# The last update of each level's outermost tile given to ScalarE and GpSimd, in the stages of three and two groups

## The reference

```python
def step(g, inp):
    ci, ni, nm, nc = inp
    local = g[:, ci, :]
    nb = g[:, ni, :]
    neigh = (nb * nm[None, :, None]).sum(axis=1) / nc
    u = jnp.concatenate([local, neigh], axis=-1)
    y_sc = jnp.tanh(u @ w1 + b1) @ w2 + b2
    g = g.at[:, ci, :].set(local + y_sc[:, None] * w_y[None, :])
    return (g, None)
```

## Time and profile before

| what | value |
|---|---|
| median of 3 runs | 4584.73 us (4581.04 to 4588.59) |
| the profiled execution | 4616.78 us, its span 4615.0 us |
| TensorE clock granted in it, mean | 0.974 |
| busy over the span | PE 4300.1, DVE 3981.3, ACT 2602.7, POOL 2142.3 us |
| scan, seven to four groups (from the first dot) | 2965.2 to 4220.5 us |
| scan, three groups (32 levels) | 4220.5 to 4396.5 us |
| scan, two groups (32 levels) | 4396.5 to 4535.6 us |
| scan, one group and the end | 4535.6 to 4615.0 us |

### The profile page before, as it was taken

How to read it: one execution, slowest core, us unless ns; L and a number is a source line. 1 busy time by engine, 2 the same in 40 slices (tenths; PEclk the granted TensorE clock), 3 DMA queues, 4 the chain that set the end, 5 groups by cost and what they waited for, 6 DMA issues and landing times. The chain is left out here.

```text
span 4615.0 us, 62189 instructions
## 1 busy us (share of the span) xinstructions
PE 4300.1 (93%) x20842; PEld 3332.0 (72%) x20842; DVE 3981.3 (86%) x5650; ACT 2602.7 (56%) x4500; POOL 2142.3 (46%) x1696
## 2 busy tenths in 40 slices
PE   5999999999999999999999999988888888889977
PEld 4888888888888888888888888744444444555555
DVE  7999999999997999999999997577777777788888
ACT  4666666666666666666666665433333333334463
POOL 1565443444343334434443434455555555555544
PEclk8999999999999999999999999998988999999999
DMA  4444444444444444444444444698898888888763
GB/s 120 146 139 145 150 138 147 138 147 144 143 143 142 145 141 147 139 146 141 146 141 140 145 140 156 217 305 275 277 280 269 259 260 257 252 244 249 214 195 114
DMA packets 254416, 835.26 MB, mean 181 GB/s; under 512 B 61706, under 2 KB 62996, under 8 KB 253972
## 3 DMA queue, kind: packets, MB, share of 16 engines
q1 hardware_dynamic: 147188, 419.02, 33.1%
q0 software_dynamic: 105776, 411.21, 23.8%
q10 hardware_dynamic: 1136, 1.05, 0.1%
HBM read 419.95 MB, written 425.85 MB: 183 GB/s over the span
## 5 line engine op out<-in xcount | busy, mean ns | idle before, releaser
L536 POOL DMA_INDIRECT s_px<-ex,wave_idx x784 | 1232.8, 1572 | 1725.2 <-ACT ex L589 1669.2
L749 DVE SCALAR_TENSOR_TENSOR dw_rows<-relu_rows,taps,dw_rows 128x1792 f32<-128x1792 f32 x872 | 1799.0, 2076 | 8.6 <-ACT relu_rows L630 8.5
L1006 PE MATMUL psum<-w_hi,u_hi 128*128 128x512 f32 x3136 | 1250.8, 399 | 30.9 <-DVE w_lo L706 18.2
L543 POOL DMA_INDIRECT out<-x_tok x897 | 905.4, 1009 | 742.1 <-DVE x_tok L832 414.7
L1007 PE MATMUL psum<-w_lo,u_hi 128*128 128x512 f32 x3136 | 1229.2, 392 | 0.0
L1008 PE MATMUL psum<-w_hi,u_lo 128*128 128x512 f32 x3136 | 1223.2, 390 | 0.0
L1027 PE MATMUL psum<-dw_rows,ident 128*128 128x512 f32 x1666 | 920.6, 636 | 61.0 <-DVE near L824 37.3
L587 ACT ACTIVATE ex<-psum 128x512 f32<-128x512 f32 x784 | 468.2, 597 | 892.4 <-PE psum L1008 885.4
L824 DVE CUSTOM_DVE_ANT_0 psum<-psum,x_tok,b_col 128x512 f32<-128x512 f32 x897 | 678.4, 756 | 325.0 <-ACT psum L647 183.8
L647 ACT ACTIVATE psum<-psum 128x512 f32<-128x512 f32 x897 | 520.8, 582 | 636.6 <-PE psum L1042 345.6
L1042 PE MATMUL psum<-u_hi,u_lo 128*128 128x512 f32 x897 | 643.2, 717 | 165.1 <-ACT u_lo L656 125.8
(11 more groups left out here) (107 smaller groups left out, 4847.8 us busy)
## 6 DMA issues: line engine op xcount, KB each, us to landing
dw_rows<-s_px SPq DMA_DIRECT2D x1230, 192.0 KB
x_tok<-x SPq DMA_DIRECT2D x112, 896.0 KB
dw_rows<-s_px SPq DMA_DIRECT2D x338, 144.0 KB
out<-x_tok POOLq DMA_INDIRECT x897
s_px<-ex,wave_idx POOLq DMA_INDIRECT x784
dw_rows<-s_px SPq DMA_DIRECT2D x112, 96.0 KB
dw_rows<-s_px SPq DMA_DIRECT2D x114, 48.0 KB
relu_rows<-coef SPq DMA_DIRECT2D x1, 5000.0 KB
```

What stands on the lines that cost most here:

```text
L536: pool.indirect_dma_start(s_px[n // (H * T)], bass.IndirectOffsetOnAxis(wave_idx[:, n:n + 1], 0), ex[:, n % OUT1_SLOTS, :], None, bounds_c ...
L543: pool.indirect_dma_start(out_rows, bass.IndirectOffsetOnAxis(store_idx[:, c:c + 1], 0), o_t[:, c % OUT_SLOTS, :], None, bounds_check=OUT_ ...
L749: dve.scalar_tensor_tensor(out=dst, in0=pair_rows(relu_rows, k + ky - 1, c, 2 * kx * NB), scalar=taps[:, c, 3 * ky + kx:3 * ky + kx + 1], ...
L1006: pe.matmul(hid, hi, w_hi[:, k, :], start=k == 0, stop=False)
```

## The change

For the tiles with g = 0 of the stages of three and two groups (`by_pool`, 32 + 32 = 64 tiles) DVE no longer makes `finish`. ACT computes wy_row times y into the tile's `o_t` slot, right after the tanh of the next tile and ahead of its other work of that iteration. POOL then adds the tile's own values in place and, after a wait for its own result, scatters the tile as before. All the other tiles are finished by DVE. SP and POOL wait on one of two counters, by who finishes the tile.

```diff
+def by_pool(c):
+    level, g = SEQ[c]
+    return live(level) in (2, 3) and g == 0
+
+def finished(c):
+    return sum(by_pool(i) == by_pool(c) for i in range(c + 1))
...
                 if c >= PX_SLOTS:
-                    sp.wait_ge(out_ready, c - PX_SLOTS + 1)
+                    sp.wait_ge(out_pool if by_pool(c - PX_SLOTS) else out_ready, finished(c - PX_SLOTS))
...
             for c in range(TILES):
-                pool.wait_ge(out_ready, c + 1)
+                if by_pool(c):
+                    pool.wait_ge(scaled, finished(c))
+                    pool.wait_ge(px_in[c % PX_SLOTS], 16 * HALVES * (c // PX_SLOTS + 1))
+                    pool.tensor_tensor(o_t[:, c % OUT_SLOTS, :], o_t[:, c % OUT_SLOTS, :], x_t[:, c % PX_SLOTS, :],
+                                       ALU.add).then_inc(out_pool, 1)
+                    pool.wait_ge(out_pool, finished(c))
+                else:
+                    pool.wait_ge(out_ready, finished(c))
                 pool.indirect_dma_start(out_rows, bass.IndirectOffsetOnAxis(store_idx[:, c:c + 1], 0),
...
                 act.activation(psum[:, c % BANKS, :], psum[:, c % BANKS, :], ACT.Tanh).then_inc(th_ready, 1)
+                if c and by_pool(c - 1):
+                    level, g = SEQ[c - 1]
+                    act.wait_ge(y_ready, c)
+                    act.wait_ge(tile_out[(c - 1) % OUT_SLOTS], 16 * ((c - 1) // OUT_SLOTS))
+                    act.activation(o_t[:, (c - 1) % OUT_SLOTS, :], wy_row, ACT.Copy,
+                                   scale=hist[:, g, PAD + level:PAD + level + 1]).then_inc(scaled, 1)
                 ahead = c + AHEAD
                 if ahead < TILES and by_act(ahead):
...
             def finish(c):
+                if by_pool(c):
+                    return
                 dve.wait_ge(y_ready, c + 1)
```

More of the change, by code:

```diff
@@ L442, in build @@
         rows_set = sem("rows_set")
-        out_ready = sem("out_ready")
+        out_ready, scaled, out_pool = sem("out_ready"), sem("scaled"), sem("out_pool")
         tile_out = [sem(f"tile_out{i}") for i in range(OUT_SLOTS)]
```

## The result

| | before | changed |
|---|---|---|
| median of 9 runs each | 4586.43 us (4576.74 to 4594.19) | 4606.31 us (4595.81 to 4626.73) |
| ratio of the changed kernel to before | | 1.0045, 95% interval 1.0031 to 1.0059 |
| stage of three groups, from the profile | 176.0 us | 173.6 us |
| stage of two groups, from the profile | 139.1 us | 157.7 us |
| usual level (median of 31), three groups | 5.324 us | 5.290 us |

The change costs 19.9 us, 14 to 27 by the interval. The single profiled execution of the changed kernel took 4596.68 us, less than the profiled one of before. Its stages of seven to four groups, in which the two programs do the same, were together 38 us shorter (from the first dot at 2966.8 to 4184.2 us, against 2965.2 to 4220.5). Those stages differ that much from one execution to the next, so whole spans of single profiles can't be compared.

The account below looks back on a forecast made before the run. The prediction took rings through several engines, not DVE, to bound the kernel. Its terms summed as 0 + 5.2 + 0 = +5.2 us, a median of 4590 us, with a range from 4580 to 4606.

Parts of the forecast that it names:

- What bounds the kernel: Step on both stages: a ring through several engines sets the pace, 5.32 us a level with three groups, 4.26 with two.
- Rings through several engines: Dependence loops over DVE, PE and ACT with three groups, nearly ACT itself with two; no finish lies on the three-group ring.
- DVE's finish removed: Step for 64 finishes in both stages: worth 0, at most 0.41 us a level with three groups.
- The rival by which DVE sets the pace: Faster rival: each level of three groups gains up to 0.41 us, 4577 or 4572 us in all; chance 0.12.
- ACT's scaling with three groups: Step, 32 times: 0.28 to 0.38 us fits ACT's idle 0.51 us before the tanh, cost 0.
- ACT's scaling with two groups: Step, 32 times between tanh and copies on the ring: 10.6 us less 5.4 of waits, net +5.2 us.
- The gross price: Cost of one ACT scaling with two groups before waits are given back: 0.33 us, between 0.28 and 0.38.
- the swallowed wait: Two groups: ACT's copy of y terms waits about 0.2 us for PE's turn, 27 times; the scaling's delay absorbs 5.4 us.
- POOL's addition: Step, 64 times, queued behind the scatter of tile g = 1: 0.56 us long, POOL keeps up, cost 0.
- What POOL's addition does to DVE: Step at three groups: addition ends 0.08 us before DVE's next y-terms piece, cost 0; upper end 10.6 us.
- The slower rival: Three groups: an addition beyond 0.64 us holds DVE's first y-terms piece, 10.6 us at 0.97, total 4600; chance 0.22.
- the prediction's own rival: Slower, through the shared path: three groups, every nanosecond of addition beyond 0.64 us holds the y-terms product; chance 0.22.

Follow-up runs that it names:

- e10: Change in the stage of two only, scaling after ACT's copy of y terms, POOL's addition after DVE's split, cast as maximum, against before: level 4.094 us, ratio 0.9987.
- e9: Kernel before with DVE's cast of the y terms written as the maximum of the tile with itself: two-group level 4.092 us, ratio 0.9979 to before.
- e1: The change in the stage of three groups only, against the kernel before: that stage 173.30 us, ratio 1.0010 (0.9992 to 1.0028).
- e6: Change in the stage of two only, ACT scales but DVE adds in place of POOL, against before: level 4.372 us, stage 143.4 us, ratio 1.0007.
- e7: Kernel before plus an unread spare POOL addition per level of two groups, queued behind a scatter: level 4.942 us, stage 160.8 us, ratio 1.0077.
- e3: Change in the stage of two only, with ACT's scaling moved after its copy of the y terms, against before: level 4.574 us, stage 150.1 us, ratio 1.0025.
- e8: Kernel before plus a spare POOL memset per level of two groups, queued behind a scatter: level 4.251 us, stage 141.0 us, ratio 0.9995.

## Why the prediction was wrong

It gave 4590 us, +5.2, and a range to 4606. Measured is 4606.3, +19.9. By its own steps:

- **What bounds the kernel: right.** Rings through several engines, not DVE. Dots followed their tanh by 0.03 us after the change as before, and e10 against e9 shows that 32 finishes off DVE are worth 0 even with all side effects gone.
- **DVE's finish removed, worth 0: right** in both stages (e1, e10). The rival by which DVE sets the pace falls with it. The 1 us that the stage of three gained fits the product, which no longer meets a scatter, and not the finish.
- **ACT's scaling with three groups, hidden: right,** but closer than it was put: it takes 0.50 us, not 0.28 to 0.38, and the gap was 0.51.
- **ACT's scaling with two groups, +5.2 us: right,** 4.3 measured (e6). The gross price of 0.33 us was 0.29; the swallowed wait was 0.17 a level, as said, though by another way: the casts moved to where scatters don't hold them.
- **POOL's addition: 0.56 us predicted, 0.75 measured.** POOL kept up, as said.
- **What POOL's addition does to DVE, 0: this step failed.** It costs 14 of the 18.6 us. Two mistakes are in it. The step was worked out for the stage of three groups, where a product follows the addition's start by 0.64 us, and there the answer, 0, came true by luck (see below). For the stage of two it wasn't worked out at all. There the timeline had what was needed: the scatter at 4461.13, and inside it the product at 4461.47. The second mistake was to count the addition's hold from its start, behind the scatter. The hold reaches back into the scatter in which the addition is queued, once what the addition waits for is done (e7, e3).
- **The slower rival named the mechanism but not the place.** It put the hold in the stage of three, at 10.6 us and a chance of 0.22. The mechanism was a two-input instruction of DVE blocked by a POOL instruction that reads SBUF and not by one that only writes, as the section that the prediction cited says (the Trainium skill, "SBUF — State Buffer", "Who interferes with whom"). e7 and e8 agree: 0.65 us with the addition in the queue, 0.17 with the memset. The range's upper end, 4606, was short because the price was 0.33 us a level at most; it was 0.42, and 0.69 in e7.

That the addition's length was underestimated did not matter, and that was luck. By the prediction's own rival everything beyond 0.64 us would hold the product of the stage of three, and the addition took 0.75. But held products end 0.79 to 0.80 us after the addition's start wherever they began (4305.80, 0.45 us into it, 0.34 long; 4271.46, 0.34 into it, 0.46 long). Less the 0.18 us that a product takes, they were let go at 0.61 to 0.62, an estimate from these rows. The usual product begins 0.62 to 0.64 us after it, just as the hold ends.

## What to carry to other kernels

An engine that is 86% busy and yet waits once per round for another is not the bound here, and taking work off it that isn't on the ring gained nothing (e10 against e9). Before work goes to GpSimd, list in each stage what VectorE does while GpSimd's instruction runs or is queued with its waits met: every VectorE instruction there with two SBUF inputs, and every cast, is a candidate for the path. Where it can't be avoided, hold the GpSimd instruction back with a semaphore until VectorE reads from PSUM; and put a new ScalarE operation where ScalarE already waits, not ahead of what others wait for.

## What the runs showed of the hardware

All times are by the profile's recorded starts and ends, and those of POOL are rough, so what POOL had begun inside a recorded scatter isn't shown.

- A POOL addition held DVE's two-input instructions before its recorded start, while it was queued behind a scatter. The product of e7 that began 0.35 us into the scatter lasted 0.65 us, to 0.01 us after the addition's start (4250.57); the changed kernel's ended 0.13 us after it (4422.51). In e8 a product 0.34 us into the scatter with a memset queued passed in 0.17, and in e3 one with the addition queued, but still waiting for ACT, passed too (4183.27).
- An operation that meets the hold late ends with the addition: the product from 4369.19 0.05 us after it, the cast from 4423.01 0.05 us after it, e3's difference from 4253.16 0.03 us after it. Each takes 0.17 to 0.18 us alone, so it was let go some 0.6 us after the addition's start, and a product that began 0.63 us after the start was not held (4255.23).
- A scatter with nothing queued behind it holds a cast by where the cast begins. In the stages of three and two groups of before and e6 the casts that began up to 0.50 us into a scatter of 0.97 us took 0.18 to 0.19 us; those that began 0.51 to 0.77 us into it ended 0.01 to 0.02 us after it. Products that began 0.1 to 0.6 us into one passed in 0.17 to 0.18 us.
- In e8 a cast that began in a scatter was let go as the scatter ended, though a memset followed at once; one that began at 4186.05, 0.02 us before a memset, was held 0.50 us, to the memset's end. The product was held by neither.
- ScalarE's scaling of 128x256 from SBUF with a scale per partition took 498 ns, where the copy of the same size in the first layer took 384; behind it the next operation started after 0.40 us.
